# A chain of attention and feed-forward parts on one core: outward products for two tiles at a time, the mix head by head, values copied inside SBUF, norms centred by TensorE

## What is computed

```python
for i in range(DEPTH):      # 6
    x = attn_layer(shift_tokens(x), Wqkv[i], q_scale[i], k_scale[i], Wo[i]) + x
    x = ffn_layer(shift_tokens(x), ln_g[i], ln_b[i], W1[i], b1[i], W2[i], b2[i]) + x
```

## Time and profile before

| | us |
|---|---|
| median of 3 runs | 1928.72 (1924.58 to 1930.95) |
| the profiled execution | 1930.89 |
| its span in the trace | 1929.1 |
| its stretch 560 to 1440, which holds most of the stack | 880, PE busy for 813.35 |

### The profile page before, as it was taken

The page is one execution under the profiler, slowest core; times in us unless marked ns, Lnnn a source line. Parts: engine busy times, 40 slices in busy tenths (PEclk is TensorE's granted clock), DMA queues, the critical chain, the costliest instruction groups (busy, mean ns, idle before and its releaser), DMA issues. The chain is left out here.

```text
span 1929.1 us, 42065 instructions
## 1 busy us (share of the span) xinstructions
PE 1614.8 (84%) x17121; PEld 1094.3 (57%) x17121; DVE 1254.7 (65%) x2359; ACT 985.0 (51%) x1853; POOL 760.8 (39%) x1082
## 2 busy tenths in 40 slices
PE   3005576998777899999999889999888999999999
PEld 1002264675645566666666666666664677666676
DVE  6847694213956788878887778888863666666311
ACT  1034133332335567657666556666654776777232
POOL 0000030100366576766776667776740333333000
PEclk6556698999979999999999999999998999999899
DMA  3000002010043433523533434433230000000111
GB/s 109 20 4 0 3 1 62 23 33 14 1 132 91 111 96 104 150 64 103 141 90 99 108 87 113 112 105 89 86 90 1 1 1 1 1 1 1 34 33 33
DMA packets 73801, 113.35 MB, mean 59 GB/s; under 512 B 16082, under 2 KB 36152, under 8 KB 73578
## 3 DMA queue, kind: packets, MB, share of 16 engines
q1 hardware_dynamic: 72794, 110.42, 20.7%
q10 hardware_dynamic: 816, 0.24, 0.1%
HBM read 83.96 MB, written 27.50 MB: 58 GB/s over the span
## 5 line engine op out<-in xcount | busy, mean ns | idle before, releaser
L1478 POOL TENSOR_TENSOR st_r<-st_r,st_t 128x512 f32<-128x512 f32 x192 | 243.8, 1274 | 212.0 <-DVE st_t L1444 212.0
L1401 PE MATMUL PS<-st_wqkv,st_xs 128*128 128x512 f32 x576 | 306.0, 616 | 12.2 <-DVE st_t L1444 7.7
L2252 POOL TENSOR_SCALAR la_p<-la_p,la_rden 128x589 f32<-128x589 f32 x64 | 112.9, 1763 | 232.9 <-DVE la_rden L2271 232.9
L1495 POOL TENSOR_TENSOR st_r<-st_r,st_gy 128x512 f32<-128x512 f32 x192 | 195.1, 1049 | 3.8
L1436 DVE TENSOR_TENSOR st_r<-PS,st_rot 128x512 f32<-128x512 f32 x192 | 129.2, 673 | 99.8 <-ACT st_sqh L1420 99.2
L1188 ACT ACTIVATE m_h<-PS 128x512 f32<-128x512 f32 x128 | 76.5, 598 | 143.0 <-PE PS L1120 143.0
L2265 DVE TENSOR_REDUCE la_nmx<-PS 128x1 f32<-128x589 f32 x128 | 92.7, 766 | 84.8 <-PE PS L2110 84.8
L1420 ACT ACTIVATE st_sqh<-PS 128x512 f32<-128x512 f32 x192 | 114.5, 597 | 57.6 <-PE PS L1401 57.0
L2217 ACT ACTIVATE la_p<-PS,la_nmx 128x589 f32<-128x589 f32 x128 | 95.2, 748 | 82.0 <-DVE la_nmx L2265 81.9
L1213 DVE SCALAR_TENSOR_TENSOR m_y<-PS,m_g,m_y 128x128 f32<-128x128 f32 x112 | 31.5, 344 | 161.0 <-PE PS L1129 161.0
L803 POOL MEMSET l_s<- 128x144 f32 x2 | 0.4, 220 | 331.7 <-DVE x L645 217.6
(11 more groups left out here) (312 smaller groups left out, 3483.2 us busy)
## 6 DMA issues: line engine op xcount, KB each, us to landing
st_v_out<-st_v SPq DMA_DIRECT2D x48, 512.0 KB, 2.6
st_vv<-st_v_out SPq DMA_DIRECT2D x96, 256.0 KB, 3.8
st_vv<-st_v_out SPq DMA_DIRECT2D x96, 192.0 KB, 4.4
st_wqkv<-in_st_wqkv SPq DMA_DIRECT2D x18, 512.0 KB, 5.8
m_w<-in_m_w SPq DMA_DIRECT2D x32, 256.0 KB, 3.2
st_vv<-st_v_out SPq DMA_DIRECT2D x72, 64.0 KB, 1.9
st_wo<-in_st_wo SPq DMA_DIRECT2D x6, 512.0 KB
st_w<-in_st_w SPq DMA_DIRECT2D x6, 341.0 KB
```

Source lines behind the costliest of these rows:

```text
L1401: pe.matmul(PS[:, 2 + m % 2, :], self.xs[:, b, P * t:P * t + P], self.wqkv[:, l % 2, k, 512 * half:512 * half + 512], start=True, stop=Tru ...
L1478: pool.tensor_tensor(r, r, self.t2[:, c % 2, :], ALU.add).then_inc(self.added, 1)
L1495: pool.tensor_tensor(r, r, y[:, 8 * c:8 * c + 8].unsqueeze(2).broadcast_to([P, 8, D2]), ALU.mult)\
L2252: pool.tensor_scalar(self.p[:, v % 2, 0, :], self.p[:, v % 2, 0, :], self.rden[:, v % 4, 0:1], None, ALU.mult).then_inc(self.scaled0, 1)
```

## The change

Four edits go together.

1. **Outward products for two tiles.** `oT` is twice as wide. `pe_wo` and `dve_wo` run in rounds with even `T` alone, that is in rounds 0 and 2, for tiles `T - 2` and `T - 1`, with 256 columns in place of 128.
2. **The mix head by head.** `vv` loses its zeros, and each product of 128 rows and 128 columns becomes two of 64 rows and 64 columns, as in `pe_scores`. PSUM is laid out by head parity; `dve_out` reads and writes accordingly.
3. **Values copied inside SBUF.** The way through DRAM goes. `sp_shift` starts 16 copies of 64 KB from `v` to `vv` (14 in the first tile of a unit). ACT, before it writes `v` again, waits for those copies and no longer for the store.
4. **Centred norms.** PE multiplies `x` by `I - 1/128`, ACT squares from PSUM, and DVE copies PSUM to `xc` behind ACT's square. The weight goes into DVE's last product and the bias to ACT. The variance goes to bank 5. The constant `centre` is loaded with the first constants (it was in a later transfer).

```diff
-            pe.matmul(PS[:, banks[b], :], const("mean"), src[:, b, :], start=True, stop=True)\
-              .then_inc(self.mean_ready, 1)
+            pe.matmul(PS[:, banks[b], :], const("centre"), src[:, b, :], start=True, stop=True)\
+              .then_inc(self.centred, 1)
...
-                    mm = pe.matmul(PS[:, banks[self.parts[0]], at:at + 1], sq[:, b, P * j:P * j + P],
+                    mm = pe.matmul(PS[:, self.VAR, at:at + 1], sq[:, b, P * j:P * j + P],
...
-                act.activation(sq[:, b, :], xc[:, b, :], ACT.Square).then_inc(self.squared, 1)
+                act.activation(sq[:, b, :], PS[:, banks[b], :], ACT.Square).then_inc(self.squared, 1)
...
+            for b in self.parts if beta is not None else ():
+                act.wait_ge(self.scaled, n("act", self.scaled))
+                act.activation(dst[:, b, :], dst[:, b, :], ACT.Identity, bias=beta).then_inc(self.normed, 1)
+        def dve_keep(self, dve, b, banks):
+            dve.wait_ge(self.squared, n("dve", self.squared))
+            dve.tensor_copy(xc[:, b, :], PS[:, banks[b], :])
...
-                self.dve_centre(dve, b, src, banks)
+                self.dve_keep(dve, b, banks)
...
-                    c.link(dve, dve.tensor_tensor(dst[:, b, :], xc[:, b, :], PS[:, banks[b], :],
-                                                  ALU.mult))
-                    dve.tensor_scalar(dst[:, b, :], dst[:, b, :], gamma, beta, ALU.mult, ALU.add)\
-                       .then_inc(self.normed, 1)
+                    dve.scalar_tensor_tensor(dst[:, b, :], xc[:, b, :], gamma, PS[:, banks[b], :], ALU.mult, ALU.mult)\
+                       .then_inc(self.scaled, 1)
...
+        def v_copy(self, sp, T, e, h, w, signal):
+            source = 4 * T + w - (1 - h)
             rows = slice(64 * e + WIN * h, 64 * e + WIN * h + WIN)
-            src = view(self.v_out, ((T % 4) * P + WIN * first) * INNER + 512 * e,
-                       [[INNER, WIN], [WIN * INNER, count], [1, 512]])
-            sp.dma_start(self.vv[rows, to:to + count, e, :], src).then_inc(self.vshift[signal], 16)
+            block = slice(WIN * (source % 4), WIN * (source % 4) + WIN)
+            sp.dma_start(self.vv[rows, 4 * (T % 2) + w, :],
+                         self.v[block, source // 4 % 2, 512 * e:512 * e + 512]).then_inc(signal, 16)
...
         def sp_shift(self, sp, T):
             t = T % self.TILES
-            at = 4 * (T % 2)
             sp.wait_ge(self.v_evac, T * 2 + 2)
-            if T >= 4:
-                sp.wait_ge(self.pv_done, T - 3)
-            sp.dma_start(self.v_out[t], self.v[:, t % 2, :]).then_inc(self.v_stored, 16)
             if T >= 2:
                 sp.wait_ge(self.pv_done, T - 1)
             if t > 0:
                 for e in range(2):
-                    self.v_load(sp, T - 1, e, 0, 3, 1, at, t)
-            sp.wait_ge(self.v_stored, T * 16 + 16)
+                    self.v_copy(sp, T, e, 0, 0, self.v_crossed[T % 2])
             for e in range(2):
-                self.v_load(sp, T, e, 1, 0, 4, at, t)
-                self.v_load(sp, T, e, 0, 0, 3, at + 1, t)
+                for w in range(4):
+                    self.v_copy(sp, T, e, 1, w, self.vshift[t])
+                    if w:
+                        self.v_copy(sp, T, e, 0, w, self.vshift[t])
...
-                    act.wait_ge(self.v_stored, T * 16 - 16)
+                    act.wait_ge(self.vshift[(T - 2) % self.TILES], ((T - 2) // self.TILES + 1) * self.OWN)
+                    act.wait_ge(*self.crossed(T - 1))
...
-            pe.wait_ge(self.vshift[t], (u + 1) * (64 if t == 0 else 96))
+            pe.wait_ge(self.vshift[t], (u + 1) * self.OWN)
+            if t:
+                pe.wait_ge(*self.crossed(T))
...
-                    mm = pe.matmul(PS[g, c // 4, P * (c % 4):P * (c % 4) + P], self.pT[:, c, g],
-                                   self.vv[:, 4 * (T % 2) + w, :, D2 * c:D2 * c + D2], start=(c % 4 == 0), stop=(c % 4 == 3),
-                                   tile_position=(0, WIN * w), skip_group_check=True)
+                    for e in range(2):
+                        keys = slice(64 * e, 64 * e + 64)
+                        mm = pe.matmul(PS[g, e, D2 * c:D2 * c + D2], self.pT[keys, c, g],
+                                       self.vv[keys, 4 * (T % 2) + w, D2 * c:D2 * c + D2], start=(c == 0), stop=(c == 7),
...
-            dve.tensor_tensor(self.on[:, :, :, :].rearrange("p (b c) e d -> p b (c e) d", b=2),
-                              PS[:, 0:2, :].rearrange("p b (h d) -> p b h d", h=8),
-                              self.rden[:, T % 2, :].rearrange("p (b h) -> p b h", b=2).unsqueeze(3)
+            dve.tensor_tensor(self.on[:, :, :, :].rearrange("p c e d -> p e c d"),
+                              PS[:, 0:2, :].rearrange("p e (c d) -> p e c d", c=8),
+                              self.rden[:, T % 2, :].rearrange("p (c e) -> p e c", e=2).unsqueeze(3)
...
-            if half == 0 and T > 0:
-                act.wait_ge(self.wo_done, T)
-            act.activation(self.oT[:, 4 * half:4 * half + 4, :], PS[:, 4 + half, :].rearrange("p (c n) -> p c n", c=4),
+            if half == 0 and T % 2 == 0 and T > 0:
+                act.wait_ge(self.wo_done, T // 2)
+            at = P * (T % 2)
+            act.activation(self.oT[:, 4 * half:4 * half + 4, at:at + P], PS[:, 4 + half, :].rearrange("p (c n) -> p c n", c=4),
...
-            if T > 0:
-                pe.wait_ge(self.xu_ready, T)
+            if T > 1:
+                pe.wait_ge(self.xu_ready, T // 2)
             if t == 1 and u > 0:
                 pe.wait_ge(self.act_ready, 3 * u)
             for c in range(8):
-                mm = pe.matmul(PS[:, 7, 0:P], self.wo[:, l % 2, c, :], self.oT[:, c, :], start=(c == 0), stop=(c == 7))
+                mm = pe.matmul(PS[:, 7, 0:2 * P], self.wo[:, l % 2, c, :], self.oT[:, c, :], start=(c == 0), stop=(c == 7))
...
-            dve.wait_ge(self.wo_done, T + 1)
-            dve.tensor_tensor(x[:, b, P * t:P * t + P], x[:, b, P * t:P * t + P], PS[:, 7, 0:P], ALU.add)\
+            dve.wait_ge(self.wo_done, T // 2 + 1)
+            both = slice(P * t - P, P * t + P)
+            dve.tensor_tensor(x[:, b, both], x[:, b, both], PS[:, 7, 0:2 * P], ALU.add)\
...
-                pe.wait_ge(self.xu_ready, min(4 * u + 5, self.N))
+                pe.wait_ge(self.xu_ready, 2 * u + 2)
...
-                if past:
+                if past and T % 2 == 0:
                     self.pe_wo(pe, T - 1)
...
-                if past:
+                if past and T % 2 == 0:
                     self.dve_wo(dve, T - 1)
...
-                    norm.dve_centre(dve, 0, x, latents.NORM_BANKS)
+                    norm.dve_keep(dve, 0, latents.NORM_BANKS)
```

More of the change, by code:

```diff
@@ L146, in build, with __init__ @@
     class Norm:
-        def __init__(self, tag, parts=(0, 1), chain=None):
-            self.parts, self.chain = parts, chain or order
-            self.mean_ready = sem(tag + "_mean_ready")
+        def __init__(self, tag, parts=(0, 1)):
+            self.parts = parts
+            self.scaled = sem(tag + "_scaled")
             self.centred = sem(tag + "_centred")
@@ L169, in build @@
         PLAIN = (5, 4)
+        VAR = 5
         def pe_mean(self, pe, b, src, src_ready, banks):
@@ L400, in ctx_pe @@
         def ctx_pe(self, pe):
-            pe.matmul(PS[:, 6, 0:B * KC], const("mean"), ctxT[:, :], start=True, stop=True).then_inc(norm.mean_ready, 1)
+            pe.matmul(PS[:, 6, 0:B * KC], const("mean"), ctxT[:, :], start=True, stop=True).then_inc(self.prod_ready, 1)
             pe.wait_ge(norm.squared, n("pe", norm.squared))
@@ L411, in ctx_dve @@
         def ctx_dve(self, dve):
-            dve.wait_ge(norm.mean_ready, n("dve", norm.mean_ready))
+            dve.wait_ge(self.prod_ready, B + 1)
             order.link(dve, dve.tensor_tensor(self.c0[:, :], ctxT[:, :], PS[:, 6, 0:B * KC], ALU.subtract))
             dve.tensor_tensor(self.c1[:, :], self.c0[:, :], self.c0[:, :], ALU.mult).then_inc(norm.squared, 1)
+            n("dve", norm.squared)
         def ctx_out_dve(self, dve):
@@ L978, in act @@
                .then_inc(self.exps, 1)
-            norm.act(act)
+            norm.act(act, beta=column("pa_ln2b"), dst=xn)
         def dve(self, dve):
@@ L1003, in dve @@
             dve.wait_ge(self.h2_ready, 2)
-            norm.dve(dve, self.h2, xn, column("pa_ln2w"), column("pa_ln2b"))
+            norm.dve(dve, xn, column("pa_ln2w"))
     class Experts:
@@ L1269, in __init__ @@
             self.on = s("on", [P, 8, 2, D2])
-            self.oT = s("oT", [P, 8, P])
+            self.oT = s("oT", [P, 8, 2 * P])
             self.gel = s("gel", [P, 2, S])
@@ L2384, in _ @@
         attend1.act(act)
-        norm.act(act, twice=True)
+        norm.act(act, twice=True, beta=column("pa_ln1b"), dst=xn)
         attend2.kv_act(act, 3)
@@ L2392, in _ @@
         stack.act(act)
-        norm.act(act, twice=True, banks=latents.NORM_BANKS)
```

(19 more changed lines are left out.)

34 lines of the change are left out of this document (18 added, 16 removed).

## The result

| | before | after |
|---|---|---|
| median, us | 1929.5 (4 runs, 1924.6 to 1931.0) | 1974.4 (4 runs, 1968.2 to 1977.8) |
| span of the profiled execution | 1929.1 | 1974.8 |
| scores of tile 0 to scores of tile 47 | 859.7 | 905.6 |
| waits for "issue" before PE, 560 to 1440 | 36.3 in 14 | 47.7 in 32 |

The change makes the kernel slower: ratio 1.0233, 95% interval 1.0205 to 1.026. It was forecast at 1919. The spans differ by 45.7 us, and the stretch between the scores of tiles 0 and 47 alone by 46.0. Outside it the two traces differ by 2.4 us more ahead of tile 0 and 2.7 less behind tile 47, which leaves nothing to see in sum.

The account below looks back on a forecast made before the run. PE through the outward products sets round 2, a DVE-exponential-square loop rounds 3 and 1, round 0 nearly ties; fetch stalls add about 45 us. +29.8 (rounds) - 33 (stalls) - 6 (norms) = -9.2 from 1928.7: 1919 us, range 1886 to 1956.

Parts of the forecast that it names:

- Fetch stalls: PE's instruction fetches wait behind value loads; stalls cost about 45 us, 12 would remain, a gain of 33.
- the drain rate: Value copies spread 1 MB over 7.1 us of starts, not 2.67 (147 GB/s), so fetches find DMA engines with gaps.
- Some 15 of 48 scores and 11 mixes coincide: Bursts meeting a block edge within about 30 instructions; each stalls 1.5 us at most, 12 us taken in all.
- Outward products in round 2, +1.55: Paired products on PE delay piece 2, its square, DVE's run and round 3's exponential: +1.55 us a unit.
- Outward products and mix in round 0, +0.93: PE reaches the turns of the probabilities 1.40 us later; the mix on PE's path gives 0.47 back.
- Rounds 1 and 3, 0: No change: DVE's and ACT's loop sets round 1, and round 3's turns wait for the exponential anyway.
- Mix, -0.47: The mix on PE takes 1.48 us in place of 1.95; the 0.47 counts only in round 0.
- small products have a floor: Rival: the mix takes 3.2 us or more, rounds 2 and 0 lose it, time passes 1955; chance 0.04.
- Value copies at 0 on the path: SP's sixteen starts, 0.45 us each, 7.1 a tile, land before ACT or the mix needs them; cost 0.
- Norms, -6: DVE's subtraction of 0.69 us leaves the chain of nine norms, 6.2 us; taken as 6, bounds 0 and 8.
- fetches stay in the way: Rival: fetch stalls still cost 45 us, giving 1952, more if mixes stall; 1907.5 + s with s stalls; chance 0.27.
- PE is the bound after all: Rival: PE sets every round, so mix and pair savings of 31 us both count, giving 1859; chance 0.12.

Follow-up runs that it names:

- small_copies: The changed kernel with each value copy moving 32 columns of 512, same number of copies, starts and waits; 1973.9 us.
- late_wo: aligned4_zeros with piece 2 ahead of the outward products on PE, and its treatment ahead of their sum on DVE; 1935.6 us.
- aligned4_zeros: The changed kernel with edit 2 undone and 73 idle products spread over four array tiles, moving block edges away from bursts of scores; 1938.7 us.
- pairs_alone: The kernel before with edit 1 alone (outward products for two tiles); 1992.9 us, ratio 1.0345.
- pool_waits: aligned4_zeros, but in round 0 GpSimd starts its four products only when DVE has made xf; 1929.1 us.
- copies_alone: The kernel before with edit 3 alone (values copied inside SBUF, zeros kept); 1915.1 us, ratio 0.9936.
- norms_alone: The kernel before with edit 4 alone (centred norms); 1923.7 us, ratio 0.9981.

## Why the prediction was wrong

Its sum was +29.8 - 33 - 6 = -9.2 us; it came to +45 or so. Step by step:

- **Fetch stalls, "gain 45 - 12 = 33": this step failed, by 41 us.** The disturbance went from 35.3 to 43.3. The reason given ("so the fetch stood behind the values", to be cured by the drain rate) was wrong as the cause and right as an aggravation. With the copies alone issue waits fell from 36.3 to 16.5 us, and the longest from 4.4 to 2.6; but taking the bytes away in small_copies changed nothing, and moving the edges took every cut away with the traffic left as it was. What decides is where the block edges fall, and here the change did harm: a second burst of 256 instructions in every tile.
- **"Some 15 of 48 scores and 11 mixes coincide":** that was the right count to make, and near the 29 cuts. Its price was wrong twice. I took a third of the scores' stalls and none of the mixes', since "the mixes are all in rounds 1 and 3, which have room". In the changed kernel rounds 1 and 3 whose mix is cut are 0.9 to 2.5 us longer than the shortest (22.41 to 23.35 for 21.53, 16.35 to 17.21 for 14.74), and three of the twelve cut mixes stand in rounds 0 and 2. And a unit of the changed kernel moves the edges by only some 14 instructions (the distances of round 0 from tile 16 on are 9, 23, 36, 50, 63, 77 and 90), so that all its rounds 0 from tile 16 to tile 40 are cut. The half clock behind a stall was in no term.
- **Outward products in round 2, +1.55:** right (+1.81 in the changed kernel, +1.68 with the pairs alone), and late_wo confirms the way.
- **Outward products and mix in round 0, +0.93: this failed too, by 1.35 us a round.** Measured +2.28 (+2.00 with the pairs alone, where 1.40 were predicted). The step followed PE alone. DVE's sum is behind the same product, its two copies then run beside GpSimd's four products at up to 1.2 us each, and PE waits for DVE later in the round. The length of round 0 follows the copies: 19.74 to 19.95 us in aligned4_zeros, where both are slow, 18.97 in pairs_alone at tiles 32 to 40, where the second alone is, 18.60 in pool_waits, where neither is. (Between the first and the last nothing else differs; pairs_alone has neither edit 3 nor edit 4.) The 18.60 are 1.63 us over before, near the 1.40 that PE's part was priced at.
- **Rounds 1 and 3, 0:** -0.73 and -0.22. DVE no longer has the sum of 0.29 us in them, but that isn't the reason: pool_waits has no such sum either and takes 22.26 in round 1 as before, and copies_alone has it and yet takes 21.57 once. Round 1 has two lengths, and why is not explained. In round 3 the pairs alone leave 14.96; only kernels with the new mix are shorter, and late_wo.
- **Mix, -0.47:** its row has 1.48 us in place of 1.95, as predicted, and "small products have a floor" is out. The value is gone in the stalls: 41 us alone.
- **Value copies at 0 on the path:** right. Neither PE nor ACT has a wait for `st_vv`. But the starts were priced too low: 0.63 us each in place of 0.45, some 10 us a tile (10.36 at tile 20) in place of 7.1.
- **Norms, -6:** measured 3.5 alone, with an interval that just reaches no change. In the changed kernel tile 0's scores start 2.4 us later than before, not earlier. Two traces can't settle it: over all runs the five kernels without this edit have that start at 577.5 to 584.8 us, thirteen of the fifteen with it at 569.6 to 575.1, and the other two, the changed kernel and norms_alone, at 580.0 and 583.8. What moves it stays open.

Of the rivals, *fetches stay in the way* came true, with its own addition ("and more if mixes stall too"). Its s counts a stall with all that follows, 45 us before; with 8 more, 1907.5 + 53 gives 1960.5. Another 8 are the rounds' own (37.9 for 29.8), and the 6 of the norms don't show in the total; that leads to 1974.5, where 1974.4 were measured. That it comes out to a tenth is luck. *PE is the bound after all* is out: between 560 and 1440 PE is busy for 763 us where it was 813, and the time grew.

The Trainium skill, Runtime: NRT & Kernel Launch ("Instruction fetch mechanics"), calls crossings mostly hidden. The runs agree where the last edge is 116 instructions or more ahead of a burst (no cut over 0.21 us) and disagree where it is 4 to 104 ahead: in the changed kernel 28 of 35 bursts are cut there, and its 29 cuts take 51.7 us from product to product.

**The version to keep** is aligned4_copies_norms: edits 3 and 4 and 145 idle products, 1886.6 us, 2.1% under before.

## What to carry to other kernels

A burst of small products can eat a block of instructions faster than the next one comes. Count the engine's instructions, find the edge from one stall that was cut, and keep the last edge ahead of each burst well over 115 instructions away, since at 114 and 115 some bursts of this case were still cut; 145 idle products in seven places were worth 19 us in an otherwise unchanged kernel. Before cutting one instruction into two to save time on the array, price the instructions themselves. And when a product is batched and moved, follow every engine behind it to its next meeting with another, and look whether the clock falls behind the place left empty.

## What the runs showed that I had not expected

- One product instruction of 64 rows and 64 columns costs 60 ns where all use one tile of the array, 18 in four by turns, 11.6 in eight.
- DVE's copy within SBUF takes 0.42 us alone and up to 1.25 us beside GpSimd's products, while DVE's operations that read PSUM keep their 0.63 to 0.69. The Trainium skill, SBUF — State Buffer ("SBUF: two separate sides"), says that such a copy needs a port pair that GpSimd uses too, and that whichever comes second is blocked until the first is done. The rows of the two copies agree: 418 and 424 ns with the two kept apart, medians of 1086 and 1173 without.
- Stalls and clock add up: after a cut with 2.4 us of idle time PE ran near half speed for over 3 us. Idle places of 1.9 us were followed by the same without a stall, in seven of ten rounds 3 of pool_waits and in four of aligned4_zeros.
